# A mean over edges as a dense product: three bfloat16 products per block of nodes become two float32r ones

## The reference, cut to what matters

```
agg = segment_sum(x[src], dst) / max(count, 1)
agg = agg / max(norm(agg), 1e-12)
out = agg @ Wl[i].T + bl[i] + (x / max(norm(x), 1e-12)) @ Wr[i].T
x   = relu(out)        (not after the third, last layer)
```

## Time and profile before

| | |
|---|---|
| time, median of 3 runs (6987.61 to 6997.77) | 6992.62 us |
| span of the profiled execution | 7889.6 us |
| the last network in it, 6540 us to the end | 1349.6 us |
| TensorE busy in the last network | 1293.52 us |
| mean granted clock of TensorE in it | 0.98 of full speed |

### The profile page before, as it was taken

How to read it: one execution, slowest core, us unless ns; L and a number is a source line. 1 busy time by engine, 2 the same in 40 slices (tenths; PEclk the granted TensorE clock), 3 DMA queues, 4 the chain that set the end, 5 groups by cost and what they waited for, 6 DMA issues and landing times. The chain is left out here.

```text
span 7889.6 us, 137900 instructions
## 1 busy us (share of the span) xinstructions
PE 6633.2 (84%) x47136; PEld 4683.6 (59%) x47136; DVE 3780.3 (48%) x11316; ACT 2080.9 (26%) x6122; POOL 2537.4 (32%) x2577
## 2 busy tenths in 40 slices
PE   4999789999978888887777877867777777999999
PEld 2555446666657777776666666645555554555555
DVE  7787534444444444443444444456666662222111
ACT  3555312222222222222333333322222220000000
POOL 0000000000035555554555555546666660000000
PEclk6999989999989999998999998955555558999999
DMA  5343442222245445444455454434444446555654
GB/s 160 107 136 113 131 131 88 89 88 86 78 124 148 144 143 145 141 141 138 138 144 145 142 144 138 138 89 126 127 125 126 126 124 201 196 193 196 200 192 160
DMA packets 669788, 1085.73 MB, mean 138 GB/s; under 512 B 247170, under 2 KB 495206, under 8 KB 667043
## 3 DMA queue, kind: packets, MB, share of 16 engines
q1 hardware_dynamic: 474722, 508.53, 21.1%
q0 software_dynamic: 147584, 438.73, 19.7%
q10 hardware_dynamic: 46784, 129.65, 4.6%
HBM read 902.64 MB, written 174.06 MB: 136 GB/s over the span
## 5 line engine op out<-in xcount | busy, mean ns | idle before, releaser
L563 POOL DMA_INDIRECT ring<-parts,src_idx x1664 | 1626.4, 977 | 1314.1 <-issue 444.7
L2695 PE MATMUL agg_ps<-sheet,big 128*128 128x448 f16 x6090 | 1182.0, 354 | 23.6 <-DMA sheet<-adj 23.6
L563 POOL DMA_INDIRECT ring<-rows_yh,src_idx x832 | 840.0, 1010 | 540.7 <-issue 226.0
L1099 ACT ACTIVATE strong<-hid,s_b 128x128 f32<-128x128 f32 x2352 | 668.3, 369 | 1160.9 <-PE hid L1208 441.1
L2695 PEld LDWEIGHTS agg_ps<-sheet,big 128*128 128x128 bf16 x6090 | 598.2, 99 | 565.8 <-DMA sheet<-adj 25.9
L1208 PE MATMUL hid<-agg,big 128*128 128x128 f32 x6272 | 806.3, 281 | 62.2 <-issue 51.6
L1208 PEld LDWEIGHTS hid<-agg,big 128*128 128x128 f32 x6272 | 774.9, 197 | 136.0 <-issue 119.1
L1196 PE MATMUL y<-big,strong 128*128 128x256 f32 x3136 | 742.8, 385 | 13.7 <-issue 12.0
L683 DVE TENSOR_TENSOR acc<-acc,sums 128x128 f32 x416 | 120.3, 289 | 1120.8 <-DMA acc<-in_edge_type 759.5
L1196 PEld LDWEIGHTS y<-big,strong 128*128 128x128 f32 x3136 | 586.4, 191 | 98.4 <-issue 18.5
L713 PE MATMUL sums<-onehot,ring 128*128 128x64 bf16 x9984 | 412.0, 196 | 174.8 <-issue 134.8
(11 more groups left out here) (443 smaller groups left out, 9757.7 us busy)
## 6 DMA issues: line engine op xcount, KB each, us to landing
sheet<-adj SPq DMA_DIRECT2D x294, 784.0 KB, 4.1
sheets<-adj SPq DMA_DIRECT2D x74, 784.0 KB, 4.2
adj<-big ACTq DMA_DIRECT2D x7, 5488.0 KB
adj<-acc ACTq DMA_DIRECT2D x7, 5488.0 KB
relb<-rel_rows ACTq DMA_DIRECT2D x106, 256.0 KB
ring<-parts,src_idx POOLq DMA_INDIRECT x1664
big<-adj SPq DMA_DIRECT2D x24, 784.0 KB, 4.7
parts<-cut SPq DMA_DIRECT2D x98, 192.0 KB, 1.9
```

Of the source, the lines that this page charges most:

```text
L563: nc.gpsimd.indirect_dma_start(ring[:, k, 0:YH] if edge_net else ring[:, k, :], None, table, bass.IndirectOffsetOnAxis(ap=src_idx[:, i * R ...
L1099: ins = nc.scalar.activation(s["strong"][:, e % 2, j, :], p["hid"][:, bank_at, j * P:(j + 1) * P], ACT.Relu, bias=self.w["s1_b"][:, e, j:j ...
L2695: ins = nc.tensor.matmul(ps[:, 0:HALF_COLS], rows_in[:, k * per + s, c, :], sheet[:, k, s * HALF_COLS:(s + 1) * HALF_COLS], start=(k == fi ...
```

## The change

In the last network a row is now two float32r halves: the row written as float32r (a 4-byte type that TensorE takes) and the rest, also written as float32r. A block takes two products instead of three. [...] A sheet is loaded once the sheet three units earlier has been copied. [...] The transposes become two products with a float32r identity. The third network no longer cuts and stores parts; at the start of the last network the halves are made on ScalarE and VectorE from the float32 rows. `far_rows` gathers float32 rows in place of `far_sums`' parts. The squares of the rows are taken from the rows as they are made. The core of the diff:

```diff
 BESIDE = 2
+STAGED = 3
+WORKED = 2
+FIRST_BLOCKS = 4
...
-                self.finish(m, 3)
+                self.finish(m, 2)
...
-                yield 15
-                m.need(self.act, "h_row")
-                self.cut_dve(m, s["h2"][:, :], s["left"][:, :], [s["cut"][:, c, :] for c in range(PARTS)])
...
-        def unit(ps, rows_in, sheet, k, first, last, some=range(NODE_BLOCKS // UNITS)):
-
-            for s in some:
-                for c in range(PARTS):
-                    ins = nc.tensor.matmul(ps[:, 0:HALF_COLS], rows_in[:, k * per + s, c, :],
-                                           sheet[:, k, s * HALF_COLS:(s + 1) * HALF_COLS],
-                                           start=(k == first and s == 0 and c == 0),
-                                           stop=(k == last and s == per - 1 and c == PARTS - 1), skip_group_check=True)
+        LAYER_UNITS = 2 * CHUNKS * UNITS
+        unit_parts = ((0, FIRST_BLOCKS), (FIRST_BLOCKS, per))
+
+        def unit_part(ps, rows_in, sheet, k, part, first, last):
+
+            lo, hi = unit_parts[part]
+            for s in range(lo, hi):
+                for c in range(2):
+                    ins = nc.tensor.matmul(ps[:, 0:HALF_COLS], rows_in[:, c, k * per + s, :],
+                                           sheet[:, s * HALF_COLS:(s + 1) * HALF_COLS], start=(k == first and s == 0 and c == 0),
+                                           stop=(k == last and s == per - 1 and c == 1), skip_group_check=True)
             return ins
 
         def dense_pass(l, w3, bufs):
...
+                        def load_sheet(n):
+                            g, k = n // UNITS % halves, n % UNITS
+                            if n - STAGED >= first:
+                                sp.wait_ge(sem["worked_a"], made(n - STAGED))
+                                sp.wait_ge(sem["worked_b"], made(n - STAGED))
+                            sp.dma_start(staged[:, n % STAGED, :], adj[g, :, k * per * HALF_COLS:(k + 1) * per * HALF_COLS]
+                                         ).then_inc(sem[f"sheet{n % STAGED}"], 16)
...
+                        def products(n, part, out, rows_in, last):
+                            k = n % UNITS
+                            pe.wait_ge(sem["worked_a" if part == 0 else "worked_b"], made(n))
+                            if l == 0 and n < UNITS and part == 0:
+                                pe.wait_ge(sem["low_in"], k + 1)
+                            unit_part(out, rows_in, worked[:, n % WORKED, :], k, part, 0, last
+                                      ).then_inc(sem["made_a" if part == 0 else "made_b"], 1)
...
-                                    pe.wait_ge(sem[f"x{b // per}"], 32)
-                                last = nc.tensor.transpose(xt_ps[:, j * P:(j + 1) * P], rows[:, b, :], ident[:, :])
+                                    pe.wait_ge(sem["low_in"], b // per + 1)
+                                for c in range(2):
+                                    last = nc.tensor.matmul(xt_ps[:, j * P:(j + 1) * P], now[:, c, b, :], bufs["identr"],
+                                                            start=(c == 0), stop=(c == 1))
                             last.then_inc(sem["xt_done"], 1)
...
+                        def high_part(k):
+                            act.wait_ge(sem[f"x{k}"], 16)
+                            nc.scalar.copy(now[:, 0, some(k), :], plain[:, some(k), :]).then_inc(sem["high_in"], 1)
+
+                        def widen(n):
+                            lo, hi = (s * HALF_COLS for s in unit_parts[1])
+                            if n >= first_load:
+                                act.wait_ge(sem[f"sheet{n % STAGED}"], landed(n))
+                            if n - WORKED >= first:
+                                act.wait_ge(sem["made_b"], made(n - WORKED))
+                            nc.scalar.copy(worked[:, n % WORKED, lo:hi], staged[:, n % STAGED, lo:hi]).then_inc(sem["worked_b"], 1)
...
+                            for k in range(UNITS):
+                                n = base + g * UNITS + k + 1
+                                if l == 0 and g == 0 and k + 1 < UNITS:
+                                    high_part(k + 1)
+                                if k == 0 and g:
+                                    sums_sq(h)
+                                if first < n < end and (g < halves or k < AHEAD - 1):
+                                    widen(n)
+                                if k == 1 and l == 0 and g < halves:
+                                    for b in blocks_of(g):
+                                        act.wait_ge(sem[f"x{b // per}"], 16)
+                                        squares(plain[:, b, :], norms[:, 0, b:b + 1], b, sem["x_sq"], waste[:, 0, :])
+                                if k == 3 and g:
+                                    roots(h)
+                                if k == 4 and g < halves:
+                                    turned(g)
+                                if k == 5 and g:
+                                    leave(h)
+                        if not last_layer:
+                            for n in range(end - BESIDE, end):
+                                widen(n)
...
+                        def low_part(k):
+                            dve.wait_ge(sem["high_in"], k + 1)
+                            nc.vector.tensor_tensor(now[:, 1, some(k), :], plain[:, some(k), :], now[:, 0, some(k), :].bitcast(FP),
+                                                    ALU.subtract).then_inc(sem["low_in"], 1)
+
+                        def widen(n):
+                            lo, hi = (s * HALF_COLS for s in unit_parts[0])
+                            if n >= first_load:
+                                dve.wait_ge(sem[f"sheet{n % STAGED}"], landed(n))
+                            if n - WORKED >= first:
+                                dve.wait_ge(sem["made_a"], made(n - WORKED))
+                            nc.vector.tensor_copy(worked[:, n % WORKED, lo:hi], staged[:, n % STAGED, lo:hi]
+                                                  ).then_inc(sem["worked_a"], 1)
...
+                            own(nc.vector.tensor_scalar(row[:, p, 0:nb, :], r[:, 0:nb, :], 0.0, None, ALU.max))
+                            own(nc.vector.tensor_copy(nxt[:, 0, blk, :], row[:, p, 0:nb, :]))
+                            nc.vector.tensor_tensor(nxt[:, 1, blk, :], row[:, p, 0:nb, :], nxt[:, 0, blk, :].bitcast(FP),
+                                                    ALU.subtract).then_inc(sem["row_done"], 1)
+
                         if not last_layer:
...
+                            for k in range(UNITS):
+                                n = base + g * UNITS + k + 1
+                                if l == 0 and g == 0 and k + 1 < UNITS:
+                                    low_part(k + 1)
+                                if g == halves and k == 0:
+                                    sums_in(h)
+                                if first < n < end and (g < halves or k < AHEAD - 1):
+                                    widen(n)
+                                if g and g < halves and k == 0:
+                                    sums_in(h)
+                                if k == 2 and g:
+                                    floors(h)
+                                if k == 3 and g:
+                                    rescaled(h)
+                                if k == 4 and g:
+                                    new_rows(h)
+                        if not last_layer:
+                            for n in range(end - BESIDE, end):
+                                widen(n)
...
+            halved = own("halved", [P, 2, 2, NODE_BLOCKS, D], FR)
+            bufs = {"rows": [halved[:, k, :, :, :] for k in range(2)],
+                    "plain": halved[:, 1, 0, :, :].bitcast(FP),
...
+                    "worked": own("worked", [P, WORKED, per * HALF_COLS], FR)[:, :, :],
+                    "identr": own("identr", [P, P], FR)[:, :],
...
-                        unit(bufs["beside_ps"][:, :], parts[l % 2], bufs["sheet"], k, AHEAD, AHEAD + BESIDE - 1)
+                        for c in range(2):
+                            unit_part(bufs["beside_ps"], bufs["rows"][l % 2], bufs["worked"][:, (l * LAYER_UNITS + k) % WORKED, :],
+                                      k, c, AHEAD, AHEAD + BESIDE - 1)
                 return products
```

More of the change, by code:

```diff
@@ L2748, in _ @@
+                        for n in range(first_load + (0 if l else STAGED), end_load):
+                            load_sheet(n)
+                            k = (n - first_load) // UNITS
+                            if last_layer and (n - first_load) % UNITS == 0 and k < UNITS:
+                                load_rows(x_rows, k)
                         if not last_layer:
-                            for k in range(UNITS):
-                                sp.wait_ge(sem[f"sheet{k}"], 16 * (halves + loads_before))
```

(2 more changed lines are left out.)

375 lines of the change are left out of this document (208 added, 167 removed).

## The result

The changed kernel takes 6708.15 us (median of 4 runs, 6703.36 to 6711.36), the kernel before 6992.07 us beside it: a ratio of 0.9592, 95% interval 0.9578 to 0.9605. The forecast was 6630 us within 6560 to 6800 and "faster" at 0.85. Direction and mechanism were right, and 78 of the 362 us forecast were not had. In the changed kernel a sheet lands as float16 in one of the 3 buffers `staged` and is copied as float32r into one of the 2 buffers `worked`, blocks 0 to 3 of a unit by VectorE (part a) and blocks 4 to 6 by ScalarE (part b); TensorE waits for each part.

The account below looks back on a forecast made before the run. TensorE's own products were taken to bound the last network. Products -362.5, transposes +16, opening -14.5, seams +9 and edge pass -10 summed to -362 us: 6992.6 to 6631, say 6630 us, range 6560 to 6800 (0.8).

Parts of the forecast that it names:

- The large rival: Last network's products: 4-byte columns cost two cycles, 0.376 us per product; +377 us, 7370 us; chance 0.10.
- the loads that aren't hidden: Rival, last network: weight loads add 0.10 us per product, making 0.29; +22 us, 7015 us; chance 0.05.
- the sheets one at a time: Rival, last network: sheet loads don't overlap, a half lasts 28.7 us; -139 us, 6853 us; chance 0.07.
- dear copies: Range's upper end: VectorE's copies of counts at 2.6 us per unit set the half, +110 us.
- The price of the product: Last network: 3962 products at 0.192 us replace 5943 at 0.189 us, -362.5 us; bounds 0.188 to 0.198 us.
- Weight loads: Last network: each 4-byte weight load is covered by 0.19 us of product and costs nothing.
- Transposes: Last network: 147 instructions become 294 products of 128 columns at 0.11 us each, +16 us.
- Copies hidden: Last network's halves: VectorE's and ScalarE's copies of counts are covered by TensorE and cost nothing.
- Sheets hidden: Last network: a sheet is due every 3.2 us, three buffers allow one per 1.8 us; no cost.
- Opening: Start of the last network: 8.8 MB at 345 GB/s, 33 instead of 47.5 us, -14.5 us.
- Seams: Between the last network's layers: the root behind a copy adds some 3 us; +4.5 us per seam, +9 us.
- The third edge pass: Pass before the last network: four cut steps per block go, 51 us of VectorE; a fifth gained, -10 us.

Follow-up runs that it names:

- small_copies: Changed kernel; after the first two units of layer 0 each copy of counts writes 8 columns instead of 1792 or 1344: 6694.89 us (one run).
- quiet: `small_copies`, and after the first three sheets each load brings 64 of 3136 columns: 42 products take 8.65 us; no total time given.
- narrow_weights: Changed kernel; each block's second product loads 32 columns of weights instead of 128: 42 products take 8.57 us; no total time given.
- narrow_columns: Changed kernel; each block's second product takes 256 of its 448 columns: 42 products take 6.81 us; no total time given.
- base: The kernel before, unedited, profiled a second time: span 6986.1 us.
- opening: Changed kernel; layer 0's loads in the order sheet n, rows n for all seven units: 6700.54 us (one run).
- seam: Changed kernel; only the next layer's first sheet loaded ahead in the dense phase, the other two beside the far rows' gathers: 6689.04 us (one run).
- two_f16_spread: Kernel before with rows as two float16 halves, and the last layer's x rows loaded one unit per half: 6608.06 us, ratio 0.9458.

## Why the prediction was right, and where its sum was off

*A price near that of 2-byte operands: right.* The large rival, 0.376 us per product and slower, is refuted by the first product measured, and with it the loads that aren't hidden (0.29 us) and the sheets one at a time (28.7 us a half; it is 23.1 with sheets at 254 GB/s). The kernel is faster because a block's three products at 0.189 us became two at 0.206. That the time fell within the range is in part luck: the range's upper end was reached by 110 us for dear copies, which didn't come, and only 24 for a dearer product, which cost 55.

*The price of the product: the term that was mis-sized.* Before, 63 products took 11.91 us, 0.189 each and 0.42 ns per column. "Pass" and "cycle" are the prediction's names for these 0.42 ns, and that a float32 column passes twice is its reading of 0.84 ns; no run shows the passes themselves. The step was "nothing but the count of passes is seen in them", by which the float32 rows gave 0.188 to 0.198 us, and 0.192 was taken. In those rows a column takes 0.84 to 0.88 ns, so a price between 0.42 and 0.84 ns could not show in them. It is 0.206 us, outside of my bounds: 3962 x 0.014 = 55 us. The experiments place it: not the copies (`small_copies`), not the sheets (`quiet`), little of the weight load (`narrow_weights`), no constant per instruction (`narrow_columns`), but 0.46 ns for each column of 4 bytes at a granted clock of 1.00. By what it comes about inside TensorE no run shows. The 0.188 us of the prediction's lower bound, 448 x 0.42, are 9% below the measurement, which decides.

*Weight loads: right for 448 columns.* Covered, but for some 4 ns, and for 73 ns more on the first product behind short ones. They come out with products of 128 and 192 columns. There each product costs 0.105 to 0.116 us. A load is listed with more, 188 to 192 ns, in the steady halves after, and with 99 ns for the bfloat16 rows of `base`.

*Transposes: right.* 294 at 0.105 us against 0.11.

*Copies hidden: right in the halves.* Without them a half changes by no more than 0.01 us. (The prediction's half of the kernel before, 31.5 us, divided by 13 a window that also holds three units of the next layer; by the squares it was 30.445. The sum didn't use it.) Not seen were 4.1 us in the opening and about 4 us at each seam, where TensorE is not the cover.

*Sheets hidden: right*, by `quiet`.

*Opening: -10.1 us by the squares, -14.5 predicted.* The term took 345 GB/s throughout, and after the change the opening moves 290. The order in SyncE's queue was not read: `opening` gets 4.8 us more, or 2 at the least.

*Seams: 22.3 us lost beyond the halves, 9 predicted.* The step that failed took the root behind a copy, "some 3 us", for the only thing that comes late. It came 2.2 us later; but the last copies also free the buffers late, and the phase ends with a sheet's landing (`seam`, 13 us for both seams). The clock was left out too. After the change, the first seam's products and the granted clock of the windows that they fill:

```profile
6037.06 5.08 PE L2695 MATMUL agg_ps<-worked,halved 128*128 128x448 f32 x14
6041.98 0.83 PE L2791 MATMUL xw_ps<-w,xt 128*128 128x128 f32 x6
```

```profile
6023.90:6031.40 7.50, 7.47 (x28) 6.86 (x29) 0.43 (x1) 0.19 (x1) 3.79 (x4) 0.74 0.14 34
6037.00:6042.00 5.00, 5.00 (x17) 4.45 (x17) 2.10 (x3) 1.69 (x2) 0.00 (x0) 0.56 0.81 251
```

Before, at the same place:

```profile
7027.33 0.51 PE L2644 MATMUL far_ps<-far_hot,far_ring 128*128 128x64 bf16 x12
7031.27 5.82 PE L2695 MATMUL agg_ps<-sheet,big 128*128 128x448 f16 x21
7036.93 0.83 PE L2767 MATMUL xw_ps<-w,xt 128*128 128x128 f32 x6
```

At granted clocks of 0.74 and 0.56 the 28 products beside (from 6023.93 to 6031.44, as shown with `seam`) take 0.27 us each and the 14 behind them 4.92 / 14 = 0.35 instead of 0.206, some 4 us together. Before, the 42 beside took (7027.33 - 7019.39) / 42 = 0.189 us at a granted clock of 1.00, and only the 21 behind them were dear, 5.66 / 21 = 0.27 us at a granted clock of 0.70, some 2 us together.

A gain at the second seam was missed altogether, 7.9 us of `x_rows` ahead of the sheets (`two_f16_spread`). Without it the seams would by this have lost 30 us.

*The third edge pass: 0, -10 predicted.* A fifth of VectorE's share was had from by_target's waits, and these rows come from the execution that was 897 us longer: 83.2 us of waits there, 13.1 in `base`. In `base` and after the pass takes 1080 us, though VectorE is busy 857.5 us in the one and 810.7 in the other. What sets the pass no run shows; VectorE's cut steps don't.

The misses are 48 us in the halves (the 55 of the products, of which some 4 come back because the intervals count 41 halves where the term counted the products of 40.4), 13 at the seams, 4 in the opening and 10 in the edge pass: 75 of the 78.

## What to carry to other kernels

Before a third product is bought off with a wider format, try another one of 2 bytes: two float16 halves take the third product away as well, need no copies, and end at 6608 us, with the loads of x spread, 1.4% below the changed kernel (with the rows of this case; no run has others). Whether the copies are needed at all no run shows: none took float16 counts beside float32r rows. When work is moved into the shadow of the bounding engine, look at the opening and the seams, where that engine stands still: there hidden microseconds come back, first as a buffer that is freed late and then as a transfer that a barrier waits for. Before a wait goes into a sum, ask whether the execution that it was read from is as long as the others: a pass of 1305 us has waits that one of 1080 hasn't. And read each queue in its order: seven loads that nobody needed yet cost 8 to 10 us at a seam, and rows ahead of a sheet 2 to 5 us in the opening.

## What the runs showed of the hardware

A float32r column costs 0.46 ns where a float16 column costs 0.42 (0.206 and 0.189 us for 448), both at a granted clock of 1.00. Taking the copies and the sheets away doesn't change the 0.206 us, and a weight load of 32 instead of 128 columns for every second product changes the mean by 2 ns. In a row of short float32r products, each with a load of 128 columns of weights, one costs 0.105 to 0.116 us: cutting 448 columns into 256 and 192 raised 0.206 to 0.232 us. At the first seam after, the granted clock was below 1.00: it was 0.79 over the 49.4 us of the seam, and 0.74 over the 28 products beside, which came after TensorE had been idle for 13.24 us and took 7.51 us from start to start (6031.44 - 6023.93), 0.27 us each.
